# A gated low-rank feed-forward layer: output columns in blocks of 512, 512 and 136 in place of 392, 384 and 384

## The reference, cut to what matters

```python
x: (128, 64, 1024)   float32, 128 batches of 64 channels
z = einsum('bct,bcd->bdt', x, cond_weights[itok])          # each batch mixes its 64 channels
result = einsum('bnd,od->bno', z, W_base) + b_base         # dense, 1024 -> 1024
logits = einsum('bnd,ed->bne', z, W_gate)                  # 8 experts
top_p, top_i = top_k(softmax(logits), 2); top_p /= sum(top_p)
route_w = sum(one_hot(top_i, 8) * top_p)
h  = einsum('bnd,erd->bner', z, A)                         # rank 16 for each expert
hw = h * route_w
delta = einsum('bner,eor->bno', hw, B)
out = x + result + delta
```

## Time and profile before

| what | us |
|---|---|
| median of 2 runs | 1025.38 (1025.07 to 1025.69) |
| span of the profiled execution, first to last instruction | 1023.8 |
| TensorE busy with matmuls | 1015.4 (99%) |
| VectorE busy | 372.2 (36%) |
| GpSimd busy | 339.2 (33%) |
| ScalarE busy | 209.5 (20%) |
| mean granted TensorE clock | 1.000 |
| moved by transfers | 107.09 MB, 105 GB/s over the span |

### The profile page before, as it was taken

How to read it: one execution, slowest core, us unless ns; L and a number is a source line. 1 busy time by engine, 2 the same in 40 slices (tenths; PEclk the granted TensorE clock), 3 DMA queues, 4 the chain that set the end, 5 groups by cost and what they waited for, 6 DMA issues and landing times.

```text
span 1023.8 us, 17244 instructions
## 1 busy us (share of the span) xinstructions
PE 1015.4 (99%) x5834; PEld 1007.7 (98%) x5834; DVE 372.2 (36%) x1240; ACT 209.5 (20%) x470; POOL 339.2 (33%) x264
## 2 busy tenths in 40 slices
PE   8999999999999999999999999999999999999998
PEld 6999999999999999999999999999999999999998
DVE  6533333333333333333333333333333333333334
ACT  6211211211122112111221221112212212122121
POOL 1424334233243342432423424324234243242331
PEclk9999999999999999999999999999999999999999
DMA  9323132232231322322213223223132232222311
GB/s 306 147 104 119 68 121 95 90 123 82 102 122 62 123 91 94 123 82 102 112 73 123 88 96 123 82 102 115 69 123 86 99 123 82 102 105 79 123 66 57
DMA packets 32009, 107.09 MB, mean 105 GB/s; under 512 B 3457, under 2 KB 6914, under 8 KB 32002
## 3 DMA queue, kind: packets, MB, share of 16 engines
q1 hardware_dynamic: 32000, 107.00, 28.5%
q10 hardware_dynamic: 2, 0.00, 0.0%
HBM read 73.43 MB, written 33.55 MB: 105 GB/s over the span
## 4 chain that ended last, share of the span: by engine, by line
PE 97%; DVE 1%; DMA 1%; SPq 1%; ACT 0%; issue 0%; DVEq 0%
PE ps_z L521 77%; PE ps_out L533 10%; PE ps_out L548 9%; DMA table_raw<-in_cond_w 1%; PE ps_hwt L541 1%; SPq L221 1%; DVE w_lo L421 0%; DVE w L462 0%; SPq L224 0%; DVE z_lo L431 0%; DVE table L484 0%; ACT table L376 0%; DVE o_sb L444 0%; SPq L234 0%; DVE pick L466 0%
## 5 line engine op out<-in xcount | busy, mean ns | idle before, releaser
L521 PE MATMUL ps_z<-w_hi,x_hi 128*128 128x384 f32 (+1 forms) x1536 | 526.0, 342 | 1.5 <-DVE w_lo L421 1.4
L521 PE MATMUL ps_z<-w_hi,x_lo 128*128 128x384 f32 (+1 forms) x1536 | 519.7, 338 | 0.0
L521 PE MATMUL ps_z<-w_lo,x_hi 128*128 128x384 f32 (+1 forms) x1536 | 519.5, 338 | 0.0
L306 POOL TENSOR_TENSOR x_lo<-xt_sb,x_hi 128x1024 fp32r<-128x1024 f32 x62 | 149.2, 2407 | 550.7 <-ACT x_hi L353 550.7
L521 PEld LDWEIGHTS ps_z<-w_hi,x_hi 128*128 128x128 f32 x1536 | 288.5, 188 | 5.7 <-DVE w_lo L421 1.9
L521 PEld LDWEIGHTS ps_z<-w_lo,x_hi 128*128 128x128 f32 x1536 | 288.7, 188 | 0.0
L521 PEld LDWEIGHTS ps_z<-w_hi,x_lo 128*128 128x128 f32 x1536 | 288.7, 188 | 0.0
L431 DVE TENSOR_TENSOR z_lo<-ps_z,z_hi 128x384 fp32r<-128x384 f32 (+1 forms) x192 | 107.6, 560 | 485.6 <-ACT z_hi L357 485.6
L357 ACT CAST z_hi<-ps_z 128x384 fp32r<-128x384 f32 (+1 forms) x192 | 92.4, 481 | 613.2 <-PE ps_z L521 612.3
L311 POOL TENSOR_TENSOR o_sb<-o_sb,bias 128x1024 f32<-128x1024 f32 x64 | 153.4, 2397 | 2.0 <-DMA o_sb<-in_x 2.0
L533 PE MATMUL ps_out<-z_hi,mix 128*128 128x384 f32 (+1 forms) x384 | 129.6, 337 | 1.1 <-POOL mix L299 0.8
(11 more groups left out here) (41 smaller groups left out, 362.0 us busy)
## 6 DMA issues: line engine op xcount, KB each, us to landing
o_sb<-in_x SPq DMA_DIRECT2D x64, 512.0 KB, 3.3
out_x<-o_sb SPq DMA_DIRECT2D x63, 512.0 KB, 2.6
xt_sb<-in_x_t SPq DMA_DIRECT2D x62, 512.0 KB, 4.4
w_raw<-in_w_t SPq DMA_DIRECT2D x8, 384.0 KB, 9.0
w_raw<-in_w_t SPq DMA_DIRECT2D x8, 196.0 KB, 4.9
xt_sb<-in_x_t SPq DMA_DIRECT2D x4, 256.0 KB, 4.8
table_raw<-in_cond_w SPq DMA_DIRECT2D x2, 256.0 KB, 8.7
b_raw<-in_b_t SPq DMA_DIRECT2D x1, 512.0 KB, 11.8
```

The lines of the kernel that those rows point to most:

```text
L306: pool.tensor_tensor(x_lo[slot][:], xt_sb[slot][:], x_hi[slot][:].bitcast(F32), ALU.subtract).then_inc(s_x_lo, 1)
L521: mm = pe.matmul(z_bank(i, c)[:, 0:width[c]], a[slot][:, k, :], w[:, k, cols(c)], start=(k == 0 and q == 0), stop=(k == KT - 1 and q == 2))
```

## The change

One line. The dense columns of the three chunks become 376, 512 and 136. With A and the gate in chunk 0, the chunks are 512, 512 and 136 columns wide in the dense and mix matmuls, and 376, 512 and 136 in the low-rank ones and in the additions to the output. The number and the order of all instructions stay; the pieces in which the weights are loaded (one slice of the inner dimension for chunk 0, two for chunks 1 and 2) get the new widths.

```diff
-BASE_COLS = [256, 384, 384]
+BASE_COLS = [376, 512, 136]
```

## The result

The changed kernel takes 1119.78 us (median of two runs, 1118.89 to 1120.66) against 1025.38: a ratio of 1.0925 with a 95% interval of 1.0904 to 1.0945. It is 94 us slower. The forecast was 1118.

What follows compares the result with a forecast made beforehand. TensorE bounds the kernel: matmul count times distance between starts, plus some 8 us of ends. 1023.8 + 94.1 + 0.9 - 0.5 - 1.5 = 1116.8 us of span; with the median 1.6 us above, 1118 us, range 1018 to 1135.

Steps and rivals of the forecast that it cites:

- The line: All TensorE matmuls: distance between starts is 0.453 ns a column plus 1 ns, so equal counts and columns take equal time.
- the end of the range at 228: 512-column matmuls: starts 228 ns apart instead of 233 if the addition to streaming stays 15 ns; up to 17 us less.
- The floor: Narrow chunk's 1920 matmuls: the next weight load keeps starts 112 ns apart instead of 63, adding 94.1 us; 67%.
- my 10% rival: Narrow chunk: the transpose is slow by itself, 136 columns start 63 ns apart, nothing is added, 1024 us; 10%.
- Four passes: Narrow chunk: at 136 columns each column needs four cycles, starts 247 ns apart, 353 us added, 1377 us; 17%.
- the halfway floor: Narrow chunk: starts 87 ns apart, 47 us added, 1071 us; 4%.
- The upper end of 117 ns: Narrow chunk: highest distance between starts allowed for 136 columns, taken from the 256-column matmuls; 104 us added.
- Due times: Transpose waiting for the gate's last product: no wait in ordinary tiles (2.2 us slack), one new 0.9 us wait in the last.
- The ends: Fill and end of the kernel: 0.5 us off for the last addition and store, 1.5 us off in the fill.

## Why the prediction was right

- **The line.** That equal counts and equal columns cost the same held with the kernel of 512, 392 and 256 columns, 1.3 us from before. 512 columns had 0.233 to 0.235 us for the line's 233 ns; the end of the range at 228 was not needed.
- **The floor.** It was the term of 94.1 us. The narrow block has 0.112 a matmul, and a tile grew by 1.48 us for a forecast of 1.47. The mechanism was right: the runs with 64 and 96 stationary columns and with bfloat16 show that the load of the next weights sets this pitch. But the row from which I took its size does not show it, and that the size fits to the nanosecond is luck. I read the turn's 0.112 us as the load that runs beneath it; with a load of half the width beneath it the turn still takes 0.10 to 0.13 us. So the premise of my 10% rival was right, the turn is slow by itself, and its conclusion was wrong: the loads of 128 float32r columns have a floor of the same size. The rows of before bound it only from above, by the 117 ns of the 256-column row.
- **Four passes** (17%) and **the halfway floor** (4%, whose 24 x 1920 ns are 46 us and not 47) are out: 0.11 us at 136 and at 192 columns. The upper end of 117 ns, from the 256-column row, is out as well: there the streaming sets the pitch.
- **Due times.** No wait in ordinary tiles, and a new one of the turn in the last tile: 1.0 us for a forecast of 0.9.
- **The ends.** This step was mis-sized. The wait in the last tile brought the clock down, which I had not priced; with the wait covered, the stretch behind it is 1.7 us shorter. In the fill the wait of the first mix went, as said, and the turn's went wholly, but TensorE waited 1.6 us for weights and ran at the 1.2 GHz level for some microseconds behind it (granted clock 0.53 from 8.4 to 11.9 us). The kernel before waited 1.4 us at the same place and kept 1.00 from 8 to 12 us. Up to the turn of tile 1 the forecast's terms give 54 x 49 ns + 1800 columns x 0.453 ns - 1.5 = 2.0 us, and it was 1.4. The sum for the span was 1116.8, and it is 1118.9. The median lies 0.9 us above the span and not 1.6, so the errors partly cancel in the 1118.

## What to carry to other kernels

When every matmul has its own stationary operand, its slot is the longer of two times: its own streaming and the load of the next weights. With 128 float32r columns that load took 112 ns, as much as the streaming of some 245 columns on this kernel's line, so a split of columns should leave no chunk narrower than that; above it, uneven chunks cost 1.3 us of 1025 here. The wait shows in no list and no busy share: compare distances between starts. And a single short matmul of another kind, here the transpose, is a weak witness for a floor, however well its number fits; a run that changes only the load says more.

## What the runs showed of the hardware that I had not expected

- The load's rate follows TensorE's granted clock. At the 1.2 GHz level the narrow float32r matmuls started 0.22 us apart, twice the 0.112, while 136 columns stream there in 113 ns. It is the same at 37 to 38 us in the run with half of the rows, in matmuls that use all 128 (0.21 us apart at a granted clock of 0.50).
- The clock fell without a gap in TensorE's work, behind narrow matmuls on 64 of the 128 rows in 16 of 61 tiles, and came back within the tile; this cost 25 us. It also fell after the single wait of 1.0 us at the end and after one of 1.6 us in the fill, while the kernel before kept 1.00 after 1.4 us.
- Going from matmuls on 128 rows to ones on 64 and back cost 0.33 us a tile at full clock.
- The transpose of 128 x 128 fp32 took some 0.11 us of TensorE between wide matmuls, and no less with a load of half the width beneath it.
- float32r matmuls of 384 columns start 15 ns above their streaming time apart, bfloat16 ones 3 ns, and a round with a change of type costs 14 ns. Where the 15 ns come from stays open: the half-width load saved 2 of them.
